# Second feed-forward product in eight matmuls: the last chunk's three terms packed in two by transfers

## The reference

```python
xn = layernorm(x)                       # x: (16, 512, 128) float32
# recurrent branch: causal depthwise conv, two gates, a scan over 512 steps
xc = conv(xn); r = sigmoid(xc @ W_r.T + b_r); i = sigmoid(xc @ W_i.T + b_i)
a = sigmoid(log_a) ** (8 * r); h = scan(a, sqrt(1 - a * a) * i * xc)
s = rmsnorm(h @ W_out.T) * gamma
# transformer branch, two layers
for l in range(2):
    h = shift_token(y); q, k, v = split(h @ wqkv[l])        # 8 heads of 64
    q, k = rotary(l2norm(q), l2norm(k))
    y = y + local_attention(q, k, v) @ wo[l]                # windows of 64
    h = layernorm(shift_token(y)) * ln_g[l] + ln_b[l]
    a, g = split(h @ w1[l] + b1[l])                         # 341 each
    y = y + (a * gelu(g)) @ w2[l] + b2[l]                   # 341 -> 128
return x + s * silu(y)
```

## Time and profile before

| | |
|---|---|
| median of 3 runs | 1276.41 us (1275.97 to 1277.53) |
| the profiled execution itself | 1274.72 us |
| its span in the profile | 1272.9 us |
| TensorE busy | 1235.6 us, 97% |
| ScalarE, GpSimd, DVE busy | 1146.8, 1113.6, 1079.3 us |
| share of the 16 DMA engines, main queue | 23.3% |
| granted TensorE clock | 0.999 |

### The profile page before, as it was taken

How to read it: one execution, slowest core, us unless ns; L and a number is a source line. 1 busy time by engine, 2 the same in 40 slices (tenths; PEclk the granted TensorE clock), 3 DMA queues, 4 the chain that set the end, 5 groups by cost and what they waited for, 6 DMA issues and landing times.

```text
span 1272.9 us, 39536 instructions
## 1 busy us (share of the span) xinstructions
PE 1235.6 (97%) x14442; PEld 1004.6 (79%) x14443; DVE 1079.3 (85%) x1921; ACT 1146.8 (90%) x3651; POOL 1113.6 (87%) x780
## 2 busy tenths in 40 slices
PE   7999999999999999999989999999999999999997
PEld 4788888888888887666767888888888888887776
DVE  7898888888888886788889999999999999984777
ACT  5899999999999999777779999999999999998886
POOL 4889999999999998479779999999999999984775
PEclk9999999999999999999999999999999999999999
DMA  5123222322233231020011222222222222211323
GB/s 172 49 62 81 72 72 77 83 74 72 73 79 79 64 81 44 26 63 1 1 30 39 48 60 60 62 57 56 57 55 56 56 60 62 50 44 35 91 76 91
DMA packets 64129, 78.59 MB, mean 62 GB/s; under 512 B 7872, under 2 KB 38144, under 8 KB 63936
## 3 DMA queue, kind: packets, MB, share of 16 engines
q1 hardware_dynamic: 63936, 76.06, 23.3%
HBM read 21.72 MB, written 4.26 MB: 20 GB/s over the span
## 4 chain that ended last, share of the span: by engine, by line
PE 84%; POOL 5%; ACT 5%; DVE 3%; issue 3%; DMA 0%; ACTq 0%; SPq 0%; DVEq 0%; POOLq 0%
PE ps L223 66%; PE ps L273 9%; PE ps L283 4%; PE ps L286 4%; POOL t L1363 2%; ACT P L720 2%; POOL hxr L1363 1%; POOL P L1363 1%; DVE t L1060 1%; PE ps L228 0%; ACT sqk L696 0%; PE ps L483 0%; DVE side L1200 0%; ACT PT L712 0%; POOL hT L1363 0%
## 5 line engine op out<-in xcount | busy, mean ns | idle before, releaser
L720 ACT ACTIVATE P<-ps,nm 128x128 f32<-128x128 f32 x1024 | 344.4, 418 | 0.0
L223 PE MATMUL ps<-wqkv,hT 128*128 128x512 f32 x1152 | 314.5, 410 | 7.3 <-DVE t L1060 5.4
L1363 POOL TENSOR_TENSOR t<-t 128x1024 f32<-128x1024 f32 x128 | 305.9, 2390 | 15.2 <-DVE t L1060 10.7
L1363 POOL TENSOR_TENSOR P<-P,rden 128x512 f32<-128x512 f32 x256 | 289.6, 1141 | 25.2 <-DVE rden L1097 21.8
L1363 POOL TENSOR_TENSOR t<-t,rr 128x1024 f32<-128x1024 f32 x128 | 243.9, 1905 | 22.9 <-ACT rr L705 21.8
L223 PEld LDWEIGHTS ps<-wqkv,hT 128*128 128x128 f32 x1152 | 201.5, 189 | 69.4 <-issue 22.3
L720 ACT ACTIVATION_READ_ACCUMULATOR P<-ps,nm 128x1 f32 x1024 | 236.1, 231 | 0.0
L1071 DVE TENSOR_TENSOR t<-ps,tabl 128x512 f32<-128x512 f32 x256 | 164.1, 682 | 38.9 <-ACT sqk L696 36.2
L1363 POOL TENSOR_TENSOR hxr<-hxf,hxr 128x512 fp32r<-128x512 f32 (+1 forms) x93 | 127.4, 1398 | 69.6 <-ACT hxr L778 69.4
L1090 DVE TENSOR_REDUCE nm<-ps 128x4 f32<-128x512 f32 x256 | 173.4, 679 | 5.7 <-PE ps L223 5.6
L712 ACT ACTIVATE PT<-ps 128x1024 f32<-128x1024 f32 x128 | 129.7, 1013 | 30.6 <-PE ps L273 30.5
(11 more groups left out here) (150 smaller groups left out, 2564.9 us busy)
## 6 DMA issues: line engine op xcount, KB each, us to landing
Vs<-Vn SPq DMA_DIRECT2D x224, 128.0 KB, 2.3
B<-rows SPq DMA_DIRECT2D x32, 256.0 KB, 3.2
side<-in_x SPq DMA_DIRECT2D x17, 256.0 KB, 3.2
A<-X SPq DMA_DIRECT2D x16, 256.0 KB, 2.5
norm<-X SPq DMA_DIRECT2D x32, 128.0 KB, 2.2
norm<-X SPq DMA_DIRECT2D x32, 127.8 KB, 2.3
hsh<-X SPq DMA_DIRECT2D x31, 128.0 KB, 2.3
hsh<-X SPq DMA_DIRECT2D x31, 127.8 KB, 2.3
```

The source lines that it names most:

```text
L223: return e.matmul(o, lhsT, rhs, start=start, stop=stop, skip_group_check=True)
L720: k = act(P[:, g, :], ps[:, 3 + s, (g % 4) * 128:(g % 4 + 1) * 128], ACT.Exp, bias=nm[:, g:g + 1], accum_out=den(s)[:, g % 4:g % 4 + 1])
L1363: return e.tensor_tensor(o, a, b_, op)
```

## The change

A matmul takes up to 128 rows, and the third chunk has 85. For the sequences 0 to 14 of both layers its three terms are put into two matmuls. The moving operand of the first holds the 85 rounded rows and under them rows 0 to 42 of the rests, its weight the 85 rounded weight rows and under them rows 0 to 42 of them again. The moving operand of the second holds the 85 rounded rows and under them rows 43 to 84 of the rests, its weight the 85 rows of the weight's rest and under them rows 43 to 84 of the rounded weight. Since no compute engine moves rows to other partitions here, three transfers per sequence do it (`pack`, on SyncE's queue): one copies the 85 rounded rows to the second operand, two put the rests under them. GpSimd writes the third chunk's rest to `lo2` (which is `hT[:, 1, 0, :]`) rather than to `hxr`, and waits until the transfers of the sequence before have landed.

The order changes too. ScalarE's splits of sequence b move into iteration b, behind `gates` and `conv` (layer 0) and around `gates2` or `rec_scale`. `down` takes the chunks 0 and 1 first with all their terms, so their rests are needed at once, and its last two matmuls wait for the transfers. On SyncE's queue the loads for layer 1 are spread between packs, and `shift_h(1, 1)` comes after all of them. The weight has a fourth piece (`w2x`), with one more load, one more ScalarE copy and one more DVE subtraction per layer.

```diff
@@ -108,11 +108,13 @@
 
         wraw1 = [B[:, (NB - 2) * L:(NB - 1) * L], B[:, (NB - 1) * L:], oT[:, 2, :]]
         gl = [side[:, 0, :], side[:, 1, :], room[:]]
+        lo2 = hT[:, 1, 0, :]
         ti = [oT[:, 0, :], oT[:, 1, :]]
         cv = [side[:, 2, :], oT[:, 3, :]]
 
         w1 = norm[:, 128:128 + 2 * HID]
         w1h = [norm[:, 128 + h * HID:128 + (h + 1) * HID] for h in range(2)]
+        w2x = norm[:, 2 * L - 128:2 * L]
         w2 = norm[:, 3 * L - 384:3 * L].rearrange("p (j d) -> p j d", j=3)
         xe = [oT[:, 0, :], oT[:, 1, :]]
         ge = [oT[:, 2, :], oT[:, 3, :]]
@@ -443,6 +446,17 @@
                     e.wait_ge(s_hxf, 3 * m + 3)
                 elif b:
                     e.wait_ge(s_xf, m)
+                if b < NB - 1:
+                    for j in range(2):
+                        e.wait_ge(s_hxhi, 3 * m + j + 1)
+                        e.wait_ge(s_hxlo, 3 * m + j + 1)
+                        for p, q in THREE:
+                            mm(ps[:, bank, :], w2r[:, q, j, :], hxr[:, b % 2, p, j, :], j == 0 and p > 0, False)
+                    e.wait_ge(s_ph[b % 2], 16 * ((8 - b % 2) * l + b // 2 + 1))
+                    e.wait_ge(s_pk, 32 * (l * (NB - 1) + b + 1))
+                    mm(ps[:, bank, :], w2r[:, 0, 2, :], hxr[:, b % 2, 0, 2, :], False, False)
+                    mm(ps[:, bank, :], w2r[0:127, 1, 2, :], hxr[0:127, b % 2, 1, 2, :], False, True).then_inc(s_y, 1)
+                    return
                 for j, (o, n) in enumerate(CH):
                     e.wait_ge(s_hxhi, 3 * m + j + 1)
                     mm(ps[:, bank, :], w2r[0:n, 1, j, :], hxr[0:n, b % 2, 0, j, :], j == 0, False)
@@ -891,10 +905,11 @@
                         e.wait_ge(s_wc, 2 * l + 2)
                         act(w1r[:, 0, :], w1, ACT.Copy).then_inc(s_whi, 1)
                     if i == (3 if l else 7):
-                        e.wait_ge(s_w2, 16 * (l + 1))
+                        e.wait_ge(s_w2, 32 * (l + 1))
                         if l:
                             e.wait_ge(s_y, NB)
-                        act(w2r[:, 0, :, :], w2, ACT.Copy).then_inc(s_w2hi, 1)
+                        act(w2r[:, 0, :, :], w2, ACT.Copy)
+                        act(w2r[:, 1, 2, :], w2x, ACT.Copy).then_inc(s_w2hi, 1)
                     if i == NT + 1:
                         e.wait_ge(s_tpk, (l + 1) * NT)
                         split_hn(l, 0)
@@ -923,14 +938,8 @@
                     rec_rms()
                 for b in range(NB + 3):
 
-                    if 0 < b < NB:
-                        split_hx(l, b - 1, 0)
-                        split_hx(l, b - 1, 1)
                     if b < NB:
                         gelu(l, b, 0)
-                    if 0 < b < NB:
-                        split_hx(l, b - 1, 2)
-                    if b < NB:
                         gelu(l, b, 1)
                     if 1 < b + 1 < NB:
                         split_hn(l, b + 1)
@@ -955,9 +964,15 @@
                             split_hx(l, b, 2)
                             e.wait_ge(s_ua, 3 * NB)
                             square(1, 0)
+                    if b < NB - 1:
+                        split_hx(l, b, 0)
+                        split_hx(l, b, 1)
+                    if l == 0 and b < NB:
                         gates2(b)
                     if l and b < NB - 1:
                         rec_scale(b)
+                    if b < NB - 1:
+                        split_hx(l, b, 2)
                     if b == 1:
                         square_mean(l, NB - 1, 7)
                     if b == 2:
@@ -1315,7 +1330,8 @@
                         e.tensor_tensor(w1r[:, 1, :], w1, w1r[:, 0, :].bitcast(F32), ALU.subtract).then_inc(s_wlo, 1)
                     if i == (4 if l else 8):
                         e.wait_ge(s_w2hi, l + 1)
-                        e.tensor_tensor(w2r[:, 1, :, :], w2, w2r[:, 0, :, :].bitcast(F32), ALU.subtract).then_inc(s_w2lo, 1)
+                        e.tensor_tensor(w2r[:, 1, 0:2, :], w2[:, 0:2, :], w2r[:, 0, 0:2, :].bitcast(F32), ALU.subtract)
+                        e.tensor_tensor(w2r[0:85, 1, 2, :], w2[0:85, 2, :], w2r[0:85, 0, 2, :].bitcast(F32), ALU.subtract).then_inc(s_w2lo, 1)
                     if l == 0 and i == NT + 2:
                         conv(0)
                     if l and i == NT + 3:
@@ -1417,6 +1433,11 @@
             def split_hx(l, b, j):
                 m, n = l * NB + b, CH[j][1]
                 e.wait_ge(s_hxhi, 3 * m + j + 1)
+                if j == 2 and b < NB - 1:
+                    if l or b:
+                        e.wait_ge(s_pk, 32 * (l * (NB - 1) + b))
+                    tt(lo2[0:n, :], hxf[0:n, j, :], hxr[0:n, b % 2, 0, j, :].bitcast(F32), ALU.subtract).then_inc(s_hxlo, 1)
+                    return
                 tt(hxr[0:n, b % 2, 1, j, :], hxf[0:n, j, :], hxr[0:n, b % 2, 0, j, :].bitcast(F32),
                    ALU.subtract).then_inc(s_hxlo, 1)
 
@@ -1537,7 +1558,8 @@
                 e.dma_start(w1, d["w1"][:, l, :]).then_inc(s_w1, 16)
 
             def load_w2(l):
-                e.dma_start(w2, d["w2"][:, l]).then_inc(s_w2, 16)
+                e.dma_start(w2, d["w2"][:, l, 0:3]).then_inc(s_w2, 16)
+                e.dma_start(w2x, d["w2"][:, l, 3]).then_inc(s_w2, 16)
 
             def shift_rows(o, x, landed):
                 e.dma_start(o[0:64, :], x[0:64, :]).then_inc(landed, 16)
@@ -1602,6 +1624,17 @@
                 if t:
                     e.dma_start(Vs[old[0], t, :], Vn[64:128, t - 1, :]).then_inc(s_vlo[t], 16)
                 e.dma_start(Vs[new[0], t, :], Vn[0:64, t, :]).then_inc(s_vhi[t], 16)
+
+            def pack(l, b):
+
+                m = l * NB + b
+                e.wait_ge(s_hxhi, 3 * m + 3)
+                first, second = hxr[:, b % 2, 0, 2, :].bitcast(F32), hxr[:, b % 2, 1, 2, :].bitcast(F32)
+                rest = lo2.bitcast(F32)
+                e.dma_start(second[0:85, :], first[0:85, :]).then_inc(s_ph[b % 2], 16)
+                e.wait_ge(s_hxlo, 3 * m + 3)
+                e.dma_start(first[85:128, :], rest[0:43, :]).then_inc(s_pk, 16)
+                e.dma_start(second[85:127, :], rest[43:85, :]).then_inc(s_pk, 16)
 
             load_x(0, xr[0], 0)
             e.dma_start(idf[:], d["idf"]).then_inc(s_idf, 16)
@@ -1644,19 +1677,26 @@
                 if l == 0:
                     e.wait_ge(s_wo, 4 * NB)
                     e.dma_start(wraw1[2], d["wqkv"][:, 1, 1024:1536]).then_inc(s_wq2, 16)
-                    keep_roots(l, NB - 1)
-                    spread_roots(l, NB - 1)
-                    e.wait_ge(s_wlo1, 3)
-                    load_tables(1, qs1)
-                    for b in range(2):
-                        shift_h(1, b)
-                    e.wait_ge(s_hn[0], NB)
-                    load_w1(1)
-                    load_w2(1)
+                    for b in range(NB - 1):
+                        pack(l, b)
+                        if b == 2:
+                            keep_roots(l, NB - 1)
+                            spread_roots(l, NB - 1)
+                        if b == 4:
+                            e.wait_ge(s_wlo1, 3)
+                            load_tables(1, qs1)
+                            shift_h(1, 0)
+                        if b == 6:
+                            e.wait_ge(s_hn[0], NB)
+                            load_w1(1)
+                            load_w2(1)
+                    shift_h(1, 1)
                 else:
                     e.wait_ge(s_wo, 8 * NB)
                     for b in range(2):
                         load_x(b, xe[b], b)
+                    for b in range(3):
+                        pack(l, b)
                     keep_roots(l, NB - 1)
                     spread_roots(l, NB - 1)
                     for b in range(NB):
@@ -1669,6 +1709,8 @@
                         e.dma_start(od[b], tiles(ge[b % 2] if b < NB - 1 else gz)).then_inc(s_out[b % 2], 16)
                         if b + 3 < NB:
                             load_x(b + 2, xe[b % 2], b % 2)
+                        if b + 3 < NB - 1:
+                            pack(l, b + 3)
                         if b == NB - 4:
                             e.wait_ge(s_hxf, 6 * NB - 1)
                             e.dma_start(tiles(xz), xd[NB - 1]).then_inc(s_xz, 16)
@@ -1735,7 +1777,7 @@
     cols = np.zeros((128, 32), np.float32)
     cols[:, 0], cols[:, 1], cols[:, 2], cols[:, 3] = a["conv_b"], a["b_r"], a["b_i"], a["log_a"]
     cols[:, 4:8] = a["conv_w"][:, 0, :]
-    w2 = np.zeros((128, DEPTH, 3, 128), np.float32)
+    w2 = np.zeros((128, DEPTH, 4, 128), np.float32)
     for l in range(DEPTH):
         c = cols[:, 8 + 9 * l:17 + 9 * l]
         c[:, 0], c[:, 1], c[:, 2] = a["ln_g"][l], a["ln_b"][l], a["b2"][l]
@@ -1743,6 +1785,8 @@
             c[:n, 3 + j] = a["b1"][l, o:o + n]
             c[:n, 6 + j] = a["b1"][l, HID + o:HID + o + n]
             w2[:n, l, j, :] = a["w2"][l, o:o + n, :]
+        w2[85:128, l, 2, :] = a["w2"][l, 256:299, :]
```

(1 more changed line is left out.)

## The result

The changed kernel takes **1374.63 us** (median of 4 runs, 1368.57 to 1382.25) against 1276.32 us for the kernel before: ratio 1.077 [1.072, 1.081], 98.3 us slower. The forecast of 1283.7 us had the sign and missed the size by 91 us, far outside its range.

The account below looks back on a forecast made before the run. TensorE, busy 97%, bounds the kernel before; afterwards the pack was to pace layer 0. Layer 0's iterations +7.45, its first +1.5, its last -0.2, layer 1 -1.8, small things +0.3: +7.25 us, 1283.7 us, range 1271.5 to 1290.

Parts of the forecast that it names:

- Part 2's landing: Layer 0's pack: the last transfer, 42 rows, lands in 2.2 us; from the rests' end to TensorE 2.8 us.
- The third split: Layer 0, ScalarE: runs after `gates2`, about 1.2 us after `up(b+1)` starts, before GpSimd's third rest wants it.
- The sum S + 4.0: Layer 0: shortest iteration that rests, transfers and TensorE's waiting matmuls allow; 8.7 us at S = 4.70.
- S: Layer 0: time of GpSimd's three rests, two of the convolution's three instructions falling on them; 4.70 us.
- DVE's loop, the second bound: Layer 0: `down_add` 0.66, `gates2` 1.12, three `hidden` 2.0, convolution 4.5 make 8.3 us, below the first bound.
- The gap named as a sign of it: A gap on TensorE before `gates` that waits for DVE would show DVE's loop as the bound, not the landing.
- Rival D: Layer 0: GpSimd and DVE block each other fully; iteration 9.3 us, total 1291.5 us; chance 0.08.
- The 1.7 us for the activation tables: Layer 0's iteration with the activation tables still stops other engines: 1.7 us on the path, between 1.0 and 2.4.
- The first iteration: Layer 0: with no second product in front of it, it meets the pack early; +1.5 us.
- Part 1: `down(b)` with eight matmuls instead of nine saves 3.47 us per layer, 6.9 in all; iteration floors 7.76 and 6.46 us.
- Part 3: Layer 1: transfers hidden by 0.5 us, 3.47 us saved less a first stall of some 1.6; -1.8 us.
- Part 4: Small things: one more ScalarE copy and DVE subtraction per layer in the attention stage, +0.3 us, between 0 and 0.6.

Follow-up runs that it names:

- sizes: The changed kernel, whole computation, with its transfers cut to 80 + 5, 42, 42 and 1 rows: 1296.22 us, ratio 1.015.
- t42: The changed kernel with 42 instead of 43 rows of rests under the first operand, one row left out: 1299.47 us, ratio 1.018.
- no_transfers: The changed kernel's order with eight matmuls and no transfers, the product of the last chunk's rest left out: 1290.32 us, ratio 1.010.
- order_nine: The changed kernel's order with the old nine matmuls, no transfers and the whole computation: 1290.62 us, ratio 1.012.
- sizes_one_input: sizes with layer 0's GpSimd rests as one-input instructions (times 0), which leaves out layer 0's rests: 1276.09 us, ratio 0.999.
- one_input: no_transfers with layer 0's GpSimd rests as full-width one-input instructions (times 0), leaving out their part of the result: 1266.45 us, ratio 0.992.

## Why the prediction was wrong

By medians, the loss in steps from run to run: the cut sizes 78.4 (change less `sizes`; 75.2 of it the one row, by `t42`), the other transfers 5.9 (`sizes` less `no_transfers`), eight matmuls for nine -0.3, the new order 14.6 (`order_nine` less before). Together 98.6 us, as steps along one path must; the medians of the kernel before beside these runs lie within 0.3 us of each other. On another path the shares can differ: GpSimd's meetings with DVE are worth 20.1 us with the transfers (`sizes` less `sizes_one_input`) and 23.9 without.

- **Part 2's landing is the step that failed.** "The pack's last transfer moves 42 rows of 2 KB (V's moves 64), so I take 2.2." The slowest is not the last but the one before it, with 43 rows: with its issue 6.1 us alone and 7.2 in place (0.61 and 6.55; what adds 1.1 there is not taken apart). The nearest row by bytes (64 rows, 2.2 us) was no bound, as time goes by the rows on one engine. From the end of the third rest to TensorE it is 7.4 us (657.13 to 664.50) where the forecast had 2.8. No rival had a landing above 2.3 us.
- **The ring was not seen.** The third split was said to be "there before GpSimd's third rest wants it". It stands behind the tanh of `gates2`, which waits for TensorE behind the pack; so each landing waits for the one before, and GpSimd stood idle for 2.36 us ahead of the third rest at 655.86. At a landing of 2.5 us this ring would be 7.6 us (an estimate, 11.6 - 6.5 + 2.5) and harmless; at 6.5 it is 11.6 us, and with the clock at half after waits the mean iteration is 172.77 / 14 = 12.3 us.
- **The sum S + 4.0 does not follow from its own terms.** It is the iteration at which TensorE no longer waits, not the one that the chain forces. The rests start at T(b) + 7.66 wherever TensorE waits in iteration b (in the changed kernel 8.58 and 9.18 us behind 641.93 and 653.87, where `up` takes 0.97 and 1.57 us more than 4.73), so a wait for the pack of b moves T(b+2) and not T(b+1). From T(b) to T(b+2) the chain takes 7.66 + S + 2.8 + 1.32, where 1.32 is 7.76 - 6.44: at S = 4.70 that is 16.5 us, 8.2 an iteration and not 8.7 (an estimate), and DVE's forecast 8.3 would have been the bound. With 7.4 for 2.8 and the 4.3 of the rests here (2.99 + 1.29) it gives 10.3, below the ring's 11.6.
- **DVE's loop, the second bound, was mis-sized.** Forecast 8.3 us: 4.5 for the convolution, 1.12 for `gates2`. Measured in `no_transfers` from start to start (586.02, 591.12, 591.78, 593.49, 595.47): 5.10 and 1.71, with 0.66 and 1.98 as forecast, 9.45 in all, the 9.44 of that iteration; the mean in `no_transfers` is 9.28. The gap named as a sign of it, `gates` waiting for DVE, is there. Rival D's iteration of 9.3 us and its 1291.5 us are what the runs with the order alone gave (1290.3 and 1290.6), though not by its rule throughout: three meetings took 5.1 us, where 1.28 + 0.75 us for each pair taken one after the other would be 6.1 (the forecast's 5.3 for three counts two pairs and a rest by itself). The `gates2` of 2.35 us beside an undisturbed rest is a meeting by that rule. Part of the nearness to 1291.5 is luck, since rival D had the pack as its bound, and these runs have none.
- **S** was forecast at 4.70 and is 5.1 (3.40 + 1.72) in `no_transfers`, 4.3 in the changed kernel; a small term. The 1.7 us for the activation tables came out right where nothing else binds: 9.24 us against 7.75 in `one_input`. The first iteration, forecast at +1.5, took 16.63 us for 9.90 in the changed kernel and 12.36 in `sizes`.
- **Issue and landing** with 42 rows: 3.34 us against 2.8, as a second issue follows after 0.84 us, not 0.53, and lands in 2.47.
- **Part 1** holds where nothing else binds: layer 1 in `no_transfers` -3.56 us against -3.47, iterations of 6.49 against 6.46.
- **Part 3**: the steady state is hidden as said (iterations alternate 6.5 and 6.8 us in `sizes`), the start is not: "a first stall" of 1.6 us is a loss of 8.3 us in the layer, +4.7 in place of -1.8. In `sizes` TensorE waits 2.19 us for the first pack, and the 18 matmuls behind it take 5.47 us.
- **Part 4**: no run parts the two small steps from the others; nothing shows them above the 0.6 us bound. That "`hidden` no longer waits for the rests" is not so in the changed kernel: at 657.14 it stood 1.15 us for the third one. The attention steps behind layer 0, with a clock of 0.75 in place of 1.00, were in no part.

## What to carry to other kernels

Before a transfer between partitions goes on the critical path, factor its row count: 41 and 43 rows went as if by one engine, and one row more or less was worth 3.6 us a transfer. If a chain waits in one iteration and releases the next but one, its length is shared by two iterations. A chain that passes through a wait on a transfer and comes back to its own issue is a ring, and costs its whole length each turn. When two-input work of GpSimd is moved, look at what DVE does at that time, and price both at the duration that they have when they meet.

## What was unexpected of the hardware

- 43 rows of 2 KB take 6.1 us, 42 take 2.4 to 2.6, 128 take 2.3.
- Two-input instructions of GpSimd and DVE mostly meet at 1.7 us each, against 1.28 and 0.75 alone; one `gates2` took 2.35 us while GpSimd's rest beside it kept its 1.28. Beside GpSimd's one-input instructions the convolution's three took 2.78 us instead of 2.32. DVE's `hidden`, with one operand in PSUM, keeps its 0.74 us beside the rests (522.95 in the kernel before, within the rests from 520.75 to 525.42).
- Part of the loss lay outside the stage that was changed: 4.6 us at a lower granted clock in the attention steps behind layer 0 of `order_nine`. It comes and goes between runs with the same order (0, 1.4 or 4.6 us).
